# Cross attention with a routed feed-forward layer on one core: transposed scores with the mask and the row maximum added by a matmul, in straight-line programs

## What is computed

```python
x = x + tanh(g_xattn[0]) * attention(layernorm(x), ctx, ctx, mask)
    # attention: q, k, v = split_heads(queries @ Wq + bq), (keys @ Wk + bk), (values @ Wv + bv)
    scores = einsum('bhqd,bhkd->bhqk', q, k) / sqrt(16)
    scores = where(mask, -1e15, scores)
    ctx = einsum('bhqk,bhkd->bhqd', softmax(scores), v);  return ctx @ Wo + bo
x = x + tanh(g_ffn[0]) * ffn(layernorm(x))
    # ffn: probs = softmax(tanh(mean(x) @ W1 + b1) @ W2 + b2); top 3 experts e with weights w
    return x + sum over the three of w[e] * (gelu(x @ Wa[e]) @ Wb[e])
```

## Time and profile before

| | |
|---|---|
| median of 3 runs | 456.11 us (451.09 to 456.2) |
| the profiled execution | 457.07 us |
| its span, first to last instruction | 455.3 us |
| attention stage, with start-up | 0 to 296.9 us |
| feed-forward stage | 296.9 to 455.3 us |
| TensorE matmul busy, whole span | 393.9 us (87%) |
| VectorE, ScalarE, GpSimd busy | 237.6, 205.7, 139.8 us |
| mean granted TensorE clock | 0.966 of 2.4 GHz |

### The profile page before, as it was taken

The page is one execution under the profiler, slowest core; times in us unless marked ns, Lnnn a source line. Parts: engine busy times, 40 slices in busy tenths (PEclk is TensorE's granted clock), DMA queues, the critical chain, the costliest instruction groups (busy, mean ns, idle before and its releaser), DMA issues. The chain is left out here.

```text
span 455.3 us, 9480 instructions
## 1 busy us (share of the span) xinstructions
PE 393.9 (87%) x2704; PEld 304.2 (67%) x2705; DVE 237.6 (52%) x611; ACT 205.7 (45%) x467; POOL 139.8 (31%) x127
## 2 busy tenths in 40 slices
PE   0729899899899889879889897789999999999996
PEld 0516677676667667657667675557777787777785
DVE  2435566886756886846887857633222222222122
ACT  1115656555446545626545555345334333344332
POOL 4452445654434644543644554100000000000000
PEclk9968999999789999989999899989999999999999
DMA  7282734735705725805734621100101101011000
GB/s 206 55 216 75 180 106 127 204 87 158 226 14 135 205 71 154 225 25 131 212 103 118 171 69 46 50 22 23 32 1 31 32 0 30 0 30 30 0 12 10
DMA packets 33919, 41.25 MB, mean 91 GB/s; under 512 B 12502, under 2 KB 28174, under 8 KB 33886
## 3 DMA queue, kind: packets, MB, share of 16 engines
q1 hardware_dynamic: 27678, 23.25, 20.5%
q0 software_dynamic: 4832, 17.11, 12.6%
q10 hardware_dynamic: 1376, 0.53, 0.5%
HBM read 33.22 MB, written 7.66 MB: 90 GB/s over the span
## 5 line engine op out<-in xcount | busy, mean ns | idle before, releaser
L976 PE MATMUL bank<-pT,vpad 125*32 125x112 f32 x768 | 90.3, 270 | 25.8 <-ACT pT L487 20.5
L479 ACT ACTIVATE probs<-probs,negmax 112x375 f32<-112x375 f32 x128 | 76.8, 601 | 60.6 <-DVE negmax L633 60.6
L976 PEld LDWEIGHTS bank<-pT,vpad 125*32 125x32 f32 x768 | 73.9, 114 | 40.7 <-ACT pT L487 29.0
L633 DVE CUSTOM_DVE_ANT_0 probs<-bank,maskb 112x375 f32<-112x375 f32 x128 | 65.0, 545 | 40.1 <-PE bank L952 30.9
L898 DVE SCALAR_TENSOR_TENSOR stage<-bank,wcur,stage 128x448 f16<-128x448 f32 x48 | 32.7, 684 | 95.6 <-ACT stage L584 95.6
L487 ACT ACTIVATE pT<-bank 125x672 f32<-125x672 f32 x64 | 46.6, 729 | 59.0 <-PE bank L961 59.0
L1140 PE MATMUL bank<-wa,ctxT 128*112 x288 | 71.5, 385 | 1.7 <-DMA ctxT<-x_scr 1.7
L1166 PE MATMUL bank<-wb,stage 128*112 x576 | 67.1, 273 | 1.4 <-DVE stage L898 1.4
L1166 PEld LDWEIGHTS bank<-wb,stage 128*112 128x112 f16 x576 | 63.5, 130 | 5.4 <-issue 1.8
L961 PE MATMUL bank<-ident,probs 112*125 112x112 f32 x384 | 61.9, 300 | 0.3 <-ACT probs L479 0.3
L961 PEld LDWEIGHTS bank<-ident,probs 112*125 112x125 f32 x384 | 49.9, 199 | 12.6 <-issue 8.4
(11 more groups left out here) (94 smaller groups left out, 350.9 us busy)
## 6 DMA issues: line engine op xcount, KB each, us to landing
stage<-in_L_ffn_Wa POOLq DMA_DIRECT2D x16, 512.0 KB, 6.0
stage<-in_L_ffn_Wb POOLq DMA_DIRECT2D x16, 512.0 KB, 4.4
ctx_s<-in_ctx SPq DMA_DIRECT2D x8, 375.0 KB
k_scr<-k_hl SPq DMA_DIRECT2D x16, 187.5 KB
kst<-k_scr SPq DMA_DIRECT2D x8, 375.0 KB, 4.4
kst<-k_scr SPq DMA_DIRECT2D x16, 187.5 KB, 4.6
q_scr<-q_hl SPq DMA_DIRECT2D x16, 112.0 KB
qst<-q_scr SPq DMA_DIRECT2D x8, 224.0 KB, 3.2
```

Of the source, the lines that this page charges most:

```text
L479: a.activation(probs[:, p % 2, e, :], probs[:, p % 2, e, :], ACT.Exp, scale=-1.0, bias=negmax[:, h:h + 1], accum_out=rowsum[:, par, h:h + ...
L633: v.tensor_tensor_reduce(out=probs[:, p % 2, e, :], in0=bank[0:SQ, 2 * (p % 2) + e, 0:SK], in1=maskb[:, par, :], scale=-1.0, scalar=3.0e38 ...
L976: ins = T.matmul(o, vpad[:, c, p, 32 * e:32 * e + 32], pT[:, p % 2, c, e * SQ:(e + 1) * SQ], start=(e == 0 and c == 0), stop=(e == 1 and c ...
```

## The change

Nearly every function is written anew. What it does:

- **Scores are computed twice.** `s1` makes them with queries in the partitions, only for the row maximum. A second set (`st_tile`) has keys in the partitions: a tile is 125 keys x 4 heads x 112 queries in one bank. A first bf16 matmul of 448 columns with a 128 x 128 identity-like matrix (`idm`) as weights adds the transposed mask (rows 0 to 124 of `mm`) and minus the maximum, which lies in three bf16 parts in rows 125 to 127 of `mm`; two f16 matmuls of 224 columns add the scores of two pairs of heads. There are 12 tiles for each batch (4 groups of two pairs, 3 thirds of the keys). ScalarE's exp of such a tile gives transposed probabilities in SBUF. `transpose_probs`, the copy L487 and the accumulated row sums are gone; the row sum is a 17th column of the values (`vp`).
- **The stacked queries are block diagonal** (`qbd`): both kinds of scores use all 128 rows of the array, with zeros for the other head.
- **The maximum** goes through `split_max` (VectorE, four small operations for half a batch), a transpose (`max_t`), a copy by ScalarE and three DMAs from SyncE for each group (`max_rows`) into rows 125 to 127.
- **The mask** is transposed once for each batch (`mask_t`), copied four times over into `mm` (`mask_tiles`, twice for each batch, 125 x 1344); fully masked batches are found by a matmul (`mask_count`) and a comparison, and zero the queries.
- **Output.** `pv` works on a group: 3 key thirds, inside them the four heads, which lie in the partitions 0, 32, 64 and 96, 17 stationary columns each. The output is copied (448 columns), transposed (4), divided by the row sums (`o_rows`), transposed back (2), projected.
- **Moved.** The f16 high part of the expert weights is made by ScalarE instead of VectorE; the chunks are 512 wide (64 of them, a ring of four). The router takes batches 0 to 5 ahead of the feed-forward stage and 6 and 7 within it. The output of batch 7, and the last transpose of batch 6, lie in the feed-forward stage.
- **Straight-line programs.** No hardware loops. Each iteration b (from -2 to 7) has four slots on each engine.

TensorE's program, and the functions the steps of the prediction speak of:

```diff
-            def transpose_probs(b, p):
-                for e in range(2):
-                    pe.wait_ge(s["act_exp"], b * NH + 2 * p + e + 1)
-                    for c in range(KC):
-                        o = PTB + c * 256 + e * SQ
-                        ins = T.transpose(flat[0:CK, o:o + SQ], probs[:, p % 2, e, c * CK:(c + 1) * CK], ident[0:SQ, 0:SQ])
-                ins.then_inc(s["pe_t"], 1)
+            def s1(b, p):
+                if there(b):
+                    if p % HP == 0:
+                        pe.wait_ge(kq_in[p // HP], 64 * (b + 1))
+                    for e in range(2):
+                        need(pe, s["dve_max"], s1_no(b, p, e) - 1)
+                        T.matmul(bank[0:SQ, e, 0:SK], qbd[:, b % 2, e, p, :], kst[:, b % 2, p * SK:(p + 1) * SK],
+                                 start=True, stop=True).then_inc(s["pe_s1"], 1)
+            def st_tile(b, g, c):
+                if there(b):
+                    t = tile(b, g, c)
+                    if c == 0:
+                        pe.wait_ge(s["mm_ready"], 2 * b + g % 2 + 1)
+                        pe.wait_ge(mmax_in[g % 2], 48 * (2 * b + g // 2 + 1))
+                    need(pe, s["act_exp"], t - len(ST_BANKS) + 1)
+                    at = ST_BANKS[t % len(ST_BANKS)]
+                    T.matmul(bank[:, at, 0:QUAD]..., idm[:, :], mm[:, g % 2, :, c, :], start=True, stop=False)
+                    for i in range(2):
+                        p = 2 * g + i
+                        w = CK if p % HP == HP - 1 and c == KC - 1 else 128
+                        ins = T.matmul(bank[0:w, at, i * 2 * SQ:(i + 1) * 2 * SQ]...,
+                                       kst[:, b % 2, p * SK + c * CK:p * SK + c * CK + w], qbd[:, b % 2, :, p, :],
+                                       start=False, stop=(i == 1))
+                    ins.then_inc(s["pe_st"], 1)
+            def pv(b, g):
+                if there(b):
+                    pe.wait_ge(s["act_exp"], tile(b, g, 2) + 1)
...
+                    for c in range(KC):
+                        for j in range(4):
+                            h = (j % 2) * PAIRS + 2 * g + j // 2
+                            ins = T.matmul(bank[32 * j:32 * j + VC, O_BANK, g * SQ:(g + 1) * SQ], vp[:, b % 2, c, h, :],
+                                           pT[:, tile(b, g, c) % PRING, j * SQ:(j + 1) * SQ], start=(c == 0), stop=(c == KC - 1))
+                    ins.then_inc(s["pe_pv"], 1)
+            for b in range(-2, B):
+                for slot in range(4):
+                    n, p = (b, 6) if slot == 0 else (b + 1, 2 * slot - 2)
+                    st_tile(b, slot, 0)
+                    s1(n, p)
+                    st_tile(b, slot, 1)
+                    pv(b if slot else b - 1, (slot - 1) % COUPLES)
+                    s1(n, p + 1)
+                    st_tile(b, slot, 2)
+                    for name in slot_uses(b, slot):
+                        put(name)
```

The other engines, around the maximum:

```diff
+            def max_rows(b, g):                      # SyncE
+                if there(b):
+                    sp.wait_ge(s["ms_done"], 2 * b + g // 2 + 1)
+                    need(sp, s["pe_st"], tile(b, g - 2, 0) + KC)
+                    for c in range(3):
...
+                        sp.dma_start(bass.AP(mm, at, [[2 * KC * QUAD, 1], [1, KC * QUAD]]),
+                                     bass.AP(ms, r * (2 * SQ) + (g // 2) * SQ, [[2 * SQ, 4], [0, KC], [1, SQ]])).then_inc(mmax_in[g % 2], 16)
+                write_k(m, 0)                        # the end of SyncE's iteration
+                write_k(m, 1)
+                max_rows(n, 0)
+                read_q(m, 0)
+                read_k(m, 0)
+                exp_tile(b, 3, 0)                    # ScalarE, slot 3
+                exp_tile(b, 3, 1)
+                exp_tile(b, 3, 2)
+                w_hi(k + 6)
+                max_copy(n, 0)
+                w_hi(k + 7)
+                row_max(n, 2)                        # VectorE, slot 2 and slot 3
+                row_max(n, 3)
+                split_max(n, 0)
+                k_lo(m, 0)
+                ln1_stats(m + 1)
+                k_lo(m, 1)
...
+                row_max(n, 4)
+                row_max(n, 5)
+                mask_tiles(n, 0)
+                residual(o)
+                ln1_apply(m + 1)
+                if b == B - 1:
+                    route_top(0)
+                ln2_apply(o)
+                if b == B - 1:
+                    route_shares(0)
```

More of the change, by code:

```diff
@@ new lines, with there, slot_uses @@
+PARTS = 8
+NPART = NZ * PARTS
+RING = 4
+PRING = 4
+ROUTES = ((0, B - 2), (B - 2, 2))
+VC = HD + 1
+ST_BANKS = (2, 3)
+O_BANK = 5
+MISC_BANKS, TAIL_BANKS = (4, 6, 7), (6, 7)
+ONE_MASKED = -(227 / 128) * 2.0 ** 49
+def there(b):
+    return 0 <= b < B
+def slot_uses(b, slot):
+    n, m, o = b + 1, b + 2, b - 1
+    every = (
+        (("V0", n), ("XT", m), ("V1", n), ("X2T", b - 2), ("MT", m), ("MX1", b)),
+        (("G", m), ("CX0", m), ("CX1", m), ("Q", m), ("OT", o)),
+        (("K0", m), ("ON", o), ("K1", m)),
+        (("MX0", n), ("OP", o)),
+    )
+    route = (None, ("H", 0), ("L", 0), ("W", 0))[slot]
+    return [u for u in every[slot] if there(u[1])] + ([route] if b == B - 1 and route else [])
@@ L982, in ctx_t @@
+            def ctx_t(name, b, t):
+                m = use(name)
                 if t == 0:
@@ new lines, in mask_t, with mask_count @@
+            def mask_t(name, b):
+                pe.wait_ge(s["mask_ready"], b + 1)
+                pe.wait_ge(s["idm_ready"], 1)
+                m = use(name).bitcast(BF16)
+                for c in range(KC):
+                    ins = T.transpose(m[0:CK, c * SQ:(c + 1) * SQ], maskb[:, b % 2, c * CK:(c + 1) * CK], idm[0:SQ, 0:SQ])
+                use_full(ins)
+            def mask_count(name, b):
+                pe.wait_ge(s["maskt_done"], b + 1)
+                m = use(name)
+                for c in range(KC):
+                    ins = T.matmul(m[:, 0:SQ], bass.AP(one_b, 0, [[1, CK], [0, 128]]), maskT[:, b % 2, c, :], start=(c == 0), stop=(c == KC - 1))
+                use_full(ins)
@@ new lines, in max_t, with o_t @@
+            def max_t(name, b, h):
+                pe.wait_ge(s["parts_done"], 2 * b + h + 1)
+                m = use(name).bitcast(BF16)
+                use_full(T.transpose(m[0:24, 0:SQ], parts[:, h, :, :].rearrange("q c h -> q (c h)"), idm[0:SQ, 0:SQ]))
+            def o_t(name, b):
+                pe.wait_ge(s["act_o"], b + 1)
+                m = use(name)
+                for g in range(COUPLES):
+                    ins = T.transpose(m[0:SQ, g * 128:(g + 1) * 128], o_sb[:, g * SQ:(g + 1) * SQ], ident[:, :])
+                use_full(ins)
@@ L1031, in o_proj, with x2_t @@
[L1031 to L1033 removed]
+                    ins = T.matmul(m[0:SQ, 0:D], tT[:, t * SQ:(t + 1) * SQ], wo_s[:, t, :], start=(t == 0), stop=(t == DT - 1))
+                use_full(ins)
+            def x2_t(name, b):
                 pe.wait_ge(s["x2_done"], b + 1)
[L1035 removed]
+                m = use(name)
                 for t in range(DT):
[L1037 to L1038 removed]
```

1472 lines of the change are left out of this document (691 added, 781 removed).

## The result

The changed kernel takes 499.19 us (median of 4 runs, 495.77 to 501.44), the kernel before 456.15 in the same comparison: a ratio of 1.0965 with a 95% interval of 1.0865 to 1.1065. The forecast of 436 is wrong in its sign. The profiled execution spans 496.8 us at a mean clock of 0.866 (before 455.3 and 0.966).

What follows compares the result with a forecast made beforehand. TensorE was taken as the fullest engine, with the gain lying before feed-forward. First tile at 47, seven periods 204.4, last iteration 23.7 and feed-forward 160.1 made a span of 435.2, forecast 436 us; range 412 to 464.

Steps and rivals of the forecast that it cites:

- What bounds it, and the period: Attention stage: TensorE is the fullest engine; a batch falls from 33.6 to 29.2 us.
- The step that failed: SyncE's issues in attention: key reads take 0.8 us each to issue, called long but early, with no wait charged.
- The slower rival: Row DMAs into `mm` land after 5.7 us instead of 2.0 before each batch's first tile: 466 us, chance 0.13.
- The wait in slot 0: TensorE at each batch's first tile waits 3.8 us for the row maxima: a 4.9 us chain against 1.1 of work.
- The clock: TensorE runs at half speed after the wait in slot 0: 1.7 us a batch, bounds 0 and 5.
- `pv`: Attention: column strips overlap by two at best, 1.5 us a group instead of 2.4, 6.0 a batch.
- The serial rival: `pv` passes do not overlap, 2.4 us a group and a period of 33: 464 us, no change; chance 0.2.
- The low bound of 4.5 a batch: Lower bound on TensorE's `pv` time in a batch, in us, against an upper bound of 9.6.
- The tiles and first scores: TensorE's score matmuls in attention: 0.38 us for a tile, 0.32 us for a pair of first scores.
- The start: Before attention: first scores at 32 us instead of 29.5, first tile at 47 after an iteration without tiles.
- The last iteration: From the end of the seven periods to feed-forward: 23.7 us, of which slot 3 with the router takes 10.4.
- Feed-forward: Last stage: 158.4 us plus 2.2 for batch 7's output work and a transpose, less 0.5 for register work: 160.1.

Runs made afterwards that it cites:

- e1: The changed kernel with its key reads cut in two by the repeat, so each source has 32 rows outermost, 8 DMAs a batch instead of 4: 432.93 us.
- e4: The kernel before with the two source dimensions of its key reads swapped, so that 2 repeats are outermost: 575.22 us, ratio 1.2771 to the kernel before.
- e6: e1 without the row DMAs that bring the maximum into `mm` and without the waits for them: 428.1 us.
- e8: e1 with the maximum in one bf16 part instead of three, so one row DMA for each group: 428.0 us.
- e9: e1 with the first half's maxima one slot earlier and the maximum in one bf16 part instead of three: 428.23 us.
- e11: e10 without the earlier maxima, that is e8 with VectorE's order changed: 423.04 us.
- e10: e9 with VectorE's second normalization and `mask_tiles` of the second half moved behind the row maxima of pairs 6 and 7: 407.59 us.

## Why the prediction was wrong, step by step

- **What bounds it, and the period.** Right that the attention stage decides and that TensorE's work falls. The period of 29.2 is e1's 29.06 and not the changed kernel's 37.4. The seven periods account for 57 of the 62 us by which the span was missed, the start for 14; the last iteration and the feed-forward stage give 3 and 6.5 back.
- **The step that failed** is a term that the sum put at nothing. The key reads entered it only as an issue of 0.8 us, "long but early"; how long they run and what they hold up had no term, although the swapped dimensions stood in the diff and the rule of the Trainium skill cited above speaks against them. What the runs show in its place: the reads run on two engines for 18 to 20 us of each batch, and the rows issued behind them reach their reader 9.3 to 11.8 us later, so TensorE also waits at slots 1 and 2 (3.9 and 3.5 us in batch 2), where the sum had no wait, and works at half speed after it. e1 and e4 show the price both ways: 66 us off the changed kernel, 118 on the one before.
- **The slower rival** named the right transfers, row DMAs that land late, but the wrong slot and the wrong reason. It priced a late landing in slot 0, from full DMA engines and the key writes ahead. There the rows are in time: 1.2 to 2.9 us, near the 2.0 of the sum. The late ones are those of slots 1 and 2, behind the key reads, with the DMA engines busy for 0.39 to 0.41 of a period. It had 0.13, as "tiny transfers" spoke against it; these tiny transfers waited for what stood before them. That the time came out on its side, beyond its 466, is partly luck.
- **The wait in slot 0**: 3.8 forecast, 4.42 to 5.05 in e1's batches 0 to 6. The issue of three row DMAs takes 2.07 us, not 1.2: the term that was too small, as its 0.38 us was read from a load of another shape. But the wait was not worth what the sum charged. e6 took it away for 5 to 8 us instead of some 40 (3.8 and 1.7 in each period), as VectorE's lateness lay behind it. "None of them passes TensorE with its waits" was right for the busy time (24 forecast, 24 measured) and wrong for the order.
- **The clock**: half speed came with each of the three waits. In batch 2 the granted clock was 0.50 from 133.4 to 138.3 us, 0.61 from 146.3 to 150.0 and 0.58 from 156.3 to 160.0; it was 0.81 over the changed kernel's periods and 0.89 over e1's. The charge of 1.7 us was of the right kind, for one such wait.
- **`pv`**: 1.5 us forecast, 0.77 at the full clock (0.70 from its start to the next block's). The serial rival (0.2) is out. The low bound of 4.5 a batch was not low enough: 3.1. The figure of the Trainium skill that the prediction cites for three strips (2.38 times one) agrees in kind: here four strips do in 96 ns what one pass took alone. The sentence of the Trainium skill cited with it, that a weight load overlaps a running matmul only when its row group differs, is not what these blocks show: all 24 passes share the row groups, and weight loads start 5 ns after the start of a pass that lasts 271 ns.
- **The tiles and first scores**: 0.38 and 0.32 us forecast; a tile takes 0.38 in the timeline of e1 and a pair of first scores 0.32. Right.
- **The start**: 32 us forecast for the first scores, 40.2 in the changed kernel (a wait of 14.2 for `kst`), 31.6 in e1. The first tile, 47 forecast, comes at 52.2 in e1; what of these 5 us is whose was not tried.
- **The last iteration**: 23.7 forecast, 20.6. The wait for the router's weights behind the residual was there (3.43 us), the rest shorter.
- **Feed-forward**: 160.1 forecast, 153.6. The term for register work, 0.5 us, was far too small if the straight-line code is the cause, which was not tried by itself (below).

That e1 lands on the forecast is partly luck: `pv` is 3 us a batch cheaper than charged, and the waits for VectorE, which had no term, take its place.

## What to carry to other kernels

Read the outermost dimension of every DMA in a diff as a cost of its own: a repeat written first left a 187.5 KB read on two of sixteen engines, and everything issued behind it waited. When a large change is slower than its work, look for a DMA share near a small multiple of one sixteenth while an engine waits for a DMA. And a wait is worth its length only if no other engine is late behind it: two waits that cover each other must be removed together, as e8, e9, e11 and e10 show.

## What the runs showed of the hardware

- A DMA with an outermost dimension of 2 used two engines (2.0 us of packet time in each us, share 0.13 when it ran alone), and rows of 8 KB issued behind it reached their reader 9.3 to 11.8 us later, against 1.2 to 2.9 us for those issued ahead of it.
- Four column strips with 17 stationary columns each ran side by side: passes of 112 fp32 columns start 6 to 7 ns apart in fours, one four in about 96 ns, the time that one pass took before.
- The feed-forward stage gained more from the change than the issue gaps of the trace of before suggested: a unit of it, with the same matmuls, takes 5.98 us (median of 23 distances) instead of 6.22, over 5 us in 24 units. That the hardware loops and register waits are the cause was not tried by itself; 192 register operations stand beside the weight loads of its first matmuls in both kernels.
- An issue of one row of `mm` on SyncE took 0.64 us (median of 96), against 0.38 for a load of 112 rows.
